# A Householder reduction interleaved with graph layers: other scalars, a later schedule, a plainer end of the turns

## The reference, cut to what matters

```python
# layer 0
h = relu(einsum('ts,bsh->bth', adj, x @ Wg0 + bg0))
h = relu(einsum('ts,bsh->bth', adj, h @ Wg1 + bg1))
for p in range(1, MAX_SKIP + 1):          # four LSTMs, over windows of p = 1, 2, 3, 4 rows
    wins = h[:, :nw * p, :].reshape(Bv * nw, p, Hd)
    last = _lstm_last(Wih[p-1], Whh[p-1], bih[p-1], bhh[p-1], wins)
    h = h.at[:, idx, :].set(last.reshape(Bv, nw, Hd))
# layer 3
L_norm = d_inv_sqrt[:, None] * (jnp.diag(deg) - A) * d_inv_sqrt[None, :]   # 64 x 64
_, U = jnp.linalg.eigh(L_norm)
```

## Time and profile before

| | |
|---|---|
| median of three runs | 2053.51 us (2052.98 to 2054.70) |
| the profiled execution | 2054.7 us, span 2051.8 us |
| PE busy | 1932.2 us, 94% of the span |
| DVE busy | 1520.7 us, 74% |
| ACT busy | 1153.5 us, 56% |
| POOL busy | 707.7 us, 34% |
| mean granted clock of TensorE | 0.972 |

### The profile page before, as it was taken

One profiled execution on the slowest core, in us unless ns is written; L12 is line 12 of the kernel. 1 busy time (PEld: TensorE's weight loads), 2 busy tenths in 40 slices (PEclk: granted clock), 3 DMA queues, 4 the chain that ended last, 5 costly groups with the idle time before them and its releaser, 6 DMA issues. The chain is left out here.

```text
span 2051.8 us, 32793 instructions
## 1 busy us (share of the span) xinstructions
PE 1932.2 (94%) x11833; PEld 1640.5 (80%) x11833; DVE 1520.7 (74%) x4011; ACT 1153.5 (56%) x1803; POOL 707.7 (34%) x1676
## 2 busy tenths in 40 slices
PE   6999999999999999999999989989699899699996
PEld 6888888888889999987887778867599534479895
DVE  5888776566566776888888879868566589789575
ACT  3555556445444445444344357647576588557575
POOL 2555552223233341000000155556544000108675
PEclk9999999999999999999999999999799999899898
DMA  2010101001000000010000043212222000004022
GB/s 95 22 31 22 52 22 42 1 1 41 1 1 1 1 1 1 1 42 1 1 0 1 1 129 113 73 31 93 72 73 71 3 1 1 11 24 134 22 73 82
DMA packets 65632, 71.16 MB, mean 35 GB/s; under 512 B 3767, under 2 KB 63294, under 8 KB 65470
## 3 DMA queue, kind: packets, MB, share of 16 engines
q1 hardware_dynamic: 65470, 69.07, 10.4%
HBM read 43.90 MB, written 25.17 MB: 34 GB/s over the span
## 5 line engine op out<-in xcount | busy, mean ns | idle before, releaser
L1977 ACT ACTIVATE l_gates<-l_acc,l_b 128x512 f32<-128x512 f32 (+1 forms) x408 | 240.4, 620 | 88.4 <-PE l_acc L475 86.5
L1875 ACT ACTIVATE l_x_hi<-hT 128x512 fp32r<-128x512 f32 (+1 forms) x144 | 101.1, 753 | 172.6 <-PE l_acc L475 172.1
L473 PE MATMUL l_acc<-l_x_hi,l_w1x_hi 128*128 128x336 f32 (+1 forms) x544 | 187.2, 344 | 3.2 <-ACT l_gates L1977 2.2
L475 PE MATMUL l_acc<-l_x_lo,l_w1x_hi 128*128 128x336 f32 (+1 forms) x544 | 188.1, 346 | 0.0
L474 PE MATMUL l_acc<-l_x_hi,l_w1x_lo 128*128 128x336 f32 (+1 forms) x544 | 188.0, 346 | 0.0
L473 PE MATMUL l_acc<-l_x_hi,l_w0x_hi 128*128 128x512 f32 x464 | 182.1, 392 | 5.5 <-ACT l_gates L1977 4.6
L474 PE MATMUL l_acc<-l_x_hi,l_w0x_lo 128*128 128x512 f32 x464 | 181.2, 391 | 0.0
L475 PE MATMUL l_acc<-l_x_lo,l_w0x_hi 128*128 128x512 f32 x464 | 181.2, 390 | 0.0
L1984 ACT ACTIVATE l_gates<-l_cell 128x512 f32<-128x512 f32 (+1 forms) x112 | 63.7, 569 | 191.1 <-DVE l_cell L2036 156.3
L244 POOL TENSOR_TENSOR bi_shifted<-bi_shifted 32x126 f32<-32x126 f32 (+61 forms) x62 | 17.7, 286 | 398.6 <-DVE bi_shifted L231 398.6
L1247 ACT ACTIVATE leaky<-sc_g 128x1024 f32<-128x1024 f32 x128 | 121.2, 1032 | 21.8 <-PE sc_g L1361 21.4
(11 more groups left out here) (519 smaller groups left out, 6328.5 us busy)
## 6 DMA issues: line engine op xcount, KB each, us to landing
xin<-in_x SPq DMA_DIRECT2D x16, 512.0 KB, 3.8
hidB<-in_x SPq DMA_DIRECT2D x16, 512.0 KB, 5.0
x<-hT SPq DMA_DIRECT2D x16, 512.0 KB, 3.1
hidB<-x SPq DMA_DIRECT2D x16, 512.0 KB, 3.9
x<-hidB SPq DMA_DIRECT2D x16, 512.0 KB, 2.9
attention_residual<-x SPq DMA_DIRECT2D x16, 512.0 KB, 3.9
out_x<-hT SPq DMA_DIRECT2D x16, 512.0 KB, 2.9
l_rawx<-in_wih SPq DMA_DIRECT2D x4, 1024.0 KB, 5.7
```

The lines of the kernel that those rows point to most:

```text
L473: t.matmul(out, left[0], right[0], start=start, stop=False)
L475: return t.matmul(out, left[0], right[1], start=False, stop=stop)
L1875: i = nc.scalar.activation(as_windows(xs[s % 2][0][:, ch, 0:bg * nw], nw), cols(p, bg, nw, group, k, ch), ACT.Copy)
L1977: i = a.activation(gates[:, j, q, 0:n], acc[:, j, q, 0:n], FUNC[q], bias=b[:, o:o + 1])
```

## The change

Three things are changed. In the reflections, DVE's front has three operations fewer (the sign, the flag and the norm) and signals `begun` as soon as the sum of squares is there; POOL's `scalars` has 13 operations instead of 9, all 13 of them up to `scaled`, where it was 8; the flag has one place instead of two. In the schedule, the first reflection is issued in half 1 of turn 2 instead of half 0, and 30 instead of 29 are issued in the turns, the last in half 0 of turn 17. In the last turns, the order of `rows_high`/`rows_low` and `tanh`/`hidden` is the same as in all other turns.

```diff
--- before.py
+++ after.py
@@ -156,8 +156,7 @@
         self.w, self.pr = (t[0:self.Q, :, :].rearrange("p a f -> p (a f)") for t in (bi.chain, bi.other))
         self.vb_col, self.w_col = take(2, self.Q), take(2, self.Q)
         self.update, self.z, self.p = take(2, N), take(16), [take(4), take(4)]
-        self.tail, self.norm, self.den, self.sign = (self.z[:, n:n + 1] for n in (0, 1, 2, 7))
-        self.flag = [self.z[:, n:n + 1] for n in (3, 15)]
+        self.tail, self.x1x1, self.den, self.flag = (self.z[:, n:n + 1] for n in range(4))
         self.rows = bi.rows
 
     def bind(self, sem):
@@ -165,36 +164,35 @@
             "begun", "scalars", "applied", "basis"))
 
     def front(self, v, dve, k):
-
 
         s, lo, x = self.on_dve, k + 1, self.v[k % 2]
         h = lo // self.Q
         if k > 1:
             dve.wait_ge(self.rotated, k - 1)
         s.after(v.transpose(x[:, h * self.Q:], self.A[:, h:, k:k + 1].to_broadcast([self.Q, 2 - h, self.Q])))
-        x1 = x[:, lo:lo + 1]
-        s.add(v.tensor_tensor_reduce(self.prod[:, lo + 1:], x[:, lo + 1:], x[:, lo + 1:], 1.0, 1e-35,
-                                     ALU.mult, ALU.add, self.tail))
-        s.after(v.tensor_scalar(self.sign, x1, 0.0, 2.0, ALU.is_ge, ALU.mult))
-        s.after(v.tensor_scalar(self.flag[k % 2], self.tail, 1e-35, -1.0, ALU.is_gt, ALU.mult))
-        v.tensor_scalar(self.norm, x1, x1, self.tail, ALU.mult, ALU.add).then_inc(self.begun, 1)
+        v.tensor_tensor_reduce(self.prod[:, lo + 1:], x[:, lo + 1:], x[:, lo + 1:], 1.0, 1e-35,
+                               ALU.mult, ALU.add, self.tail).then_inc(self.begun, 1)
 
     def scalars(self, g, pool, k):
 
 
         s, z, lo = self.on_pool, self.z, k + 1
-        x1, norm, den, flag = self.v[k % 2][:, lo:lo + 1], self.norm, self.den, self.flag[k % 2]
-        y, t, root, r, e, half = (z[:, n:n + 1] for n in (4, 5, 6, 8, 9, 10))
+        x1, tail, norm, den, flag = self.v[k % 2][:, lo:lo + 1], self.tail, self.x1x1, self.den, self.flag
+        y, t, root, sign, r, u, half = (z[:, n:n + 1] for n in range(4, 11))
         pool.wait_ge(self.begun, k + 1)
-        s.add(g.tensor_scalar(e, flag, 1.0, x1, ALU.add, ALU.mult))
+        s.add(g.tensor_scalar(sign, x1, 0.0, 2.0, ALU.is_ge, ALU.mult))
+        s.after(g.tensor_scalar(norm, x1, x1, tail, ALU.mult, ALU.add))
+        s.add(g.tensor_scalar(flag, tail, 1e-35, -1.0, ALU.is_gt, ALU.mult))
         s.after(g.tensor_tensor(y, norm, half, ALU.pow))
+        s.add(g.tensor_scalar(root, y, norm, None, ALU.mult))
         s.after(g.tensor_scalar(t, y, y, norm, ALU.mult, ALU.mult))
         s.after(g.tensor_scalar(t, t, -0.5, 1.5, ALU.mult, ALU.add))
-        s.after(g.tensor_scalar(root, norm, y, t, ALU.mult, ALU.mult))
-        s.after(g.tensor_scalar(r, self.sign, -1.0, root, ALU.add, ALU.mult))
-        s.after(g.tensor_scalar(den, r, x1, norm, ALU.mult, ALU.add))
-        g.tensor_tensor(x1, x1, r, ALU.add).then_inc(self.scaled, 1)
-        s.after(g.tensor_scalar(self.rows[0:self.Q, 1, lo:lo + 1], r, flag, e, ALU.mult, ALU.add))
+        s.after(g.tensor_scalar(root, t, root, None, ALU.mult))
+        s.after(g.tensor_scalar(r, sign, -1.0, root, ALU.add, ALU.mult))
+        s.add(g.tensor_scalar(den, r, x1, norm, ALU.mult, ALU.add))
+        s.after(g.tensor_tensor(u, x1, r, ALU.add))
+        s.after(g.tensor_scalar(self.rows[0:self.Q, 1, lo:lo + 1], u, flag, x1, ALU.mult, ALU.add))
+        g.tensor_copy(x1, u).then_inc(self.scaled, 1)
 
     def back_products(self, v, dve, k):
 
@@ -207,7 +205,7 @@
         p, w = self.p[k % 2], N - lo
         s.after(v.tensor_tensor(self.products[:, h0:, lo:], self.AM[:, h0:, lo:],
                                 x[:, lo:].unsqueeze(1).to_broadcast([self.Q, 4 - h0, w]), ALU.mult))
-        s.add(v.tensor_scalar(self.z[:, 12:13], self.z[:, 11:12], self.flag[k % 2], None, ALU.mult))
+        s.add(v.tensor_scalar(self.z[:, 12:13], self.z[:, 11:12], self.flag, None, ALU.mult))
         s.after(v.tensor_reduce(p[:, h0:], self.products[:, h0:, lo:], AX.X, ALU.add))
         s.after(v.transpose(self.pr[:, h0 * self.Q:], p[:, h0:2].unsqueeze(2).to_broadcast([self.Q, 2 - h0, self.Q])))
         s.add(v.tensor_scalar(vb[:, lo:], x[:, lo:], self.z[:, 12:13], None, ALU.mult))
@@ -478,7 +476,7 @@
 BIAS_ROWS = 96
 BEHIND = 3
 
-REFLECTION_AT = {at: k for k, at in enumerate([(it, half) for it in range(2, 16) for half in range(2)] + [(16, 0)])}
+REFLECTION_AT = {at: k for k, at in enumerate([(2, 1)] + [(it, half) for it in range(3, 17) for half in range(2)] + [(17, 0)])}
 XBUFS = 2
 
 
@@ -1517,18 +1515,13 @@
                     input_high(it + 1)
                 if it - 1 < GROUPS:
                     second_high(it - 1)
-                if it == TURNS - 1:
-                    lstm.rows_high(act, g + 1)
                 if g >= 0:
                     lstm.gates(act, g, 0)
-                if 0 <= g < GROUPS - 2:
                     lstm.tanh(act, g, 0)
                 if 0 <= it - 2 < GROUPS:
                     rows_out(it - 2)
-                if 0 <= g + 1 < GROUPS:
+                if g + 1 >= 0:
                     lstm.rows_high(act, g + 1)
-                if g >= GROUPS - 2:
-                    lstm.tanh(act, g, 0)
                 if it < GROUPS:
                     first_high(it)
                 if g >= 0:
@@ -1602,19 +1595,15 @@
                 reflection((it, 0))
                 if it - 1 < GROUPS:
                     second_low(it - 1)
-                if it == TURNS - 1:
-                    lstm.rows_low(dve, g + 1)
                 if g >= 0:
                     lstm.cell(dve, g, 0)
                 if it + 1 < GROUPS:
                     input_low(it + 1)
-                if 0 <= g < GROUPS - 2:
+                if g >= 0:
                     lstm.hidden(dve, g, 0)
                 reflection((it, 1))
-                if 0 <= g + 1 < GROUPS:
+                if g + 1 >= 0:
                     lstm.rows_low(dve, g + 1)
-                if g >= GROUPS - 2:
-                    lstm.hidden(dve, g, 0)
                 if it < GROUPS:
                     first_low(it)
                 if g >= 0:
```

## The result

The changed kernel takes 2082.11 us (median of four runs, 2081.22 to 2083.29), the kernel before 2053.61 on the same measure. The ratio is 1.0139, with a 95% interval of 1.0121 to 1.0156: 28.5 us slower. The forecast was 15.9 us slower with a range that ended at 2081. The direction was right, the size was not, and the time lies just above the range.

A forecast was written before the change was run, and what follows sets the result against it. PE bounded the turns before; after, DVE and POOL's loop would, at 21.2 us against 20.27. Terms 11.4 - 4.1 + 4.4 + 4.5 + 1.7 - 2 = +15.9 us on 2054.7 give 2070.6, median 2069.4 us; range 2056 to 2081.

The forecast's parts named there:

- The bound: In the middle turns: DVE and POOL together become the bound, a loop of 21.2 us against PE's 20.27.
- The turns: Turns 4 to 16: the longer loop costs 0.9 us a turn, +11.4 us over 12 turns, bounds +1 and +20.
- X: DVE's stretch from a front's end to the next reciprocal, with `rows_low`, `first_low`, cell, hidden, `mixed_low`: 6.0 us before, 6.65 forecast.
- Y: DVE's stretch between reflections with `second_low`, cell, `input_low` and hidden: 5.5 us before, 6.85 forecast.
- if the flag is caught already: Upper case for Y: POOL's flag, ahead of `pow`, is held by DVE's SBUF operations, making Y 7.1 us.
- the second rival: In the turns, POOL is caught more often: loop 21.8 us, +20 there, 2079 us in all; chance 0.14.
- The start: Up to turn 4: with the reflection ahead of `second_low` in turn 2 gone, -4.1 us stay (-3.5 to -4.6).
- too short for the clock: PE's stop of 2.36 us at 56.65 shrinks to about 1.1, without half clock behind it, saving another 1.7.
- The end of the turns: Late reflections delay `rows_low` of groups 14 and 15: PE stops 4.4 and 4.5 us, plus 1.7 at half clock.
- The LSTMs: Behind the turns: PE's stops at rounds' ends move to other units and nearly cancel, -2 us (-4 to 0).
- gets out of the way: Last unit of the fourth LSTM, where 10 bisection steps fall away: part of the -2 us for the LSTMs.

The follow-up runs named there:

- short scalars: Changed kernel's schedule and order with the reflections' scalars of the kernel before: 1.0037, +7.6 us against the kernel before.
- the late start: Kernel before without the reflection ahead of `second_low` in turn 2, half 0, 28 in the turns: 0.9993, and 0.9998 when run again.
- the kernel with the ending short: Changed kernel with POOL's second half as before, 11 operations up to `scaled` instead of 13, no copy: 1.0061, +12.5 us against the kernel before.

## Why the prediction was wrong in size

**The bound: right.** DVE and POOL together are the bound in the turns. Both stretches wait for POOL, and PE waits for `h_lo`. Adding operations on POOL alone brings the long turns, and taking some off brings most of the short ones back.

**The turns: the step that failed.** I wrote "I get 6.2 if pow isn't caught, 7.0 if everything is. I take 6.65" for X and "with the hand-over 6.85" for Y, and a loop of 21.2 us. Measured in a middle turn are 6.89 and 7.20, and 2 x 3.79 + 6.89 + 7.20 = 21.67 us. Both ends had been worked out (X 7.0; "if the flag is caught already, 7.1"), and I chose between them by the assumption that `pow` would be the one caught, just as the cell starts.

What failed is the time at which POOL reaches `pow`. Sign, norm and flag had 0.75 us from the first start to that of `pow`; where nothing holds them they take 0.94 (228.28 to 229.22). The cell was put at 1.06 us behind the accumulator and starts at 1.07. The flag starts at 1.00 and would run to 1.23. By the prediction's own figures it would have run to 1.13, so it was in flight there too when the cell began, and the prediction went past that. When `pow` is caught its own work is over when the hold ends; when the flag is, `pow` is still to come. Late in the turns the reflections are shorter, the flag gets through, and `pow` is the one held:
```profile
303.06 0.23 POOL L185 TENSOR_SCALAR bi_shifted<-bi_shifted 32x1 f32<-32x1 f32 x1
303.37 2.67 POOL L186 TENSOR_TENSOR bi_shifted<-bi_shifted 32x1 f32<-32x1 f32 x1
```
Y takes 6.89 us in that turn. So the forecast's 6.85 was right for the case that it assumed, and the case was another until then; the price is 0.3 us a turn. X is longer by 0.24 for the same reason: `pow` is reached at 2.38 us instead of 2.1, 0.11 behind the start of the cell. Putting the flag behind `pow` does not win the 0.3 back in Y, since the flag's own time then falls behind the hold. That one operation is held until hidden's end, and that most of a chain then follows, sets the bulk of Y in every case.

The loop of the second rival (21.8) is what the turns show, and its "+20" is the measured +18.7. By the spans the sum was missed by 11.2 us (27.1 less 15.9), and 7.3 of them lie here. The forecast had 0.9 us for each of twelve turns, with an allowance for the first. Eleven of them became 1.5 us longer on average. The twelfth, from turn 15 to 16, was only 17.68 us for PE before and takes 19.87, 2.2 more: the loop did not shrink with PE's work.

The first turns are the other part. The reflection is longer there, and X takes 7.17 since the flag is held in it too, for 0.9 us. So three turns take 22.3 to 22.4, and the turn does not come near 21.5 until the second half. I had 0.25 us a reflection for this.

**The start: nearly right, with two terms wrong.** -3.4 for -4.1. The forecast let PE get 6.7 us ahead, 3.4 of them from two half-clock stretches that would go. Neither gain came: the stop of 1.30 us, which was to be "too short for the clock", went along with 6.8 us at 1.2 GHz, as much as in both stretches before. The stops alone gave 2.19 and 1.06 us. The result hardly suffered, since the next `h_lo` comes a whole loop and a weight split later anyway, as the prediction said (23.4 us behind the one before; it had put 22.8).

**The end of the turns: right in place, mis-sized in parts.** +11.8 for +10.6. The stops were put at 4.4 and 4.5 us, and a half-clock stretch at 1.7. Measured are 4.9 more (5.90 less 0.98) and 2.15, with half-clock stretches of 6.8 and 3.4 us. The first begins within the stop, PE is busy for 6.1 and 3.4 us of them and loses half of that, 4.7: 11.8 in all. The second stop was forecast too long and the clock's part too small. With short scalars the two stops are 4.5 and 1.5 us. The reflection in turn 17 delays by the way predicted: with the old order its stop is gone and the end is 4.0 us shorter.

**The LSTMs: mis-sized.** -2 forecast, 0.0 in the two profiles. That stops would move to other units came out; that the last unit "gets out of the way" brought nothing that the profiles show.

**The sum of the parts.** Alone, the three parts cost 16.8, 2.1 and 1.2, together 20.1 us; the whole costs 28.5, 8.4 more, where the four intervals, taken as independent, leave about 6 open. Adding the schedule to the scalars brings 6.8 instead of 2.1, adding the order to both another 4.9 instead of 1.2. The intervals of these times overlap; that the order costs something here is read from the end of the turns, 48.0 us as against 44.0. A reflection at the end of the turns stands ahead of a low part that PE waits for, so a longer chain is paid there in full, while in the middle part of it is covered.

**What stays open.** Two runs of the late start could not show its 3.4 us at the start in the whole time, and the time of schedule with order has two clusters, 2058 and 2063, of which only the lower has a profile. What lets an operation of POOL get through beside DVE, and after which stop PE's clock falls, stay open as well; the rows are below.

## What to carry to other kernels

Add up the loop of the two engines that hand work to each other, against the busiest engine's turn, before calling either of them "idle": here DVE was 80% busy and POOL 57% in a turn, and the loop had some 0.5 to 1 us to spare. (This is an estimate from the kernel before with two operations added, some 1.1 us more in a turn: its turns go from 20.95 to 20.32 us, so 0.5 us of it were covered in the early turns and nearly all in the last.) Lengthening a chain on one of them is nearly free until the slack is used and then costs its full length each turn, so cost an edit at both ends, and give the dear one its weight where the row nearest to it (an operation held for 2.71 us) shows that it happens already. Parts that are harmless alone (a place at the end of the schedule, an order of the last turns) should be timed together with the part that makes their chain longer.

## What the runs showed of the hardware that I had not expected

A GpSimd operation on a 32x1 operand that starts just ahead of a VectorE operation with two SBUF inputs can be held until a whole run of such operations has ended: the flag at 216.85 for 2.57 us, over three operations of DVE (it takes 0.23 us otherwise), and with `pow` in its place, at 216.18, for 2.92 (otherwise 0.56). A head start of 0.07 or 0.08 us did not protect it. A longer one did in the same two kernels, over the turns before the last two. Flags and `pow`s that start 0.01 to 0.12 us ahead of the cell are all held, those of 0.13 to 0.16 us go either way, and from 0.17 us on, as with the `pow` at 228.39, all get through. But the head start alone does not decide it either. In the kernel before, this operation starts 0.32 us ahead of the cell (199.03) and takes 1.04 us instead of 0.33, and so in twelve turns one after the other.
```profile
198.71 1.04 POOL L191 TENSOR_SCALAR bi_shifted<-bi_shifted 32x1 f32<-32x1 f32 x1
```
The Trainium skill (SBUF — State Buffer, "SBUF: two separate sides") says that whichever of the two starts first gets the port pair for its whole instruction. By that rule the flag at 216.85 and `pow` at 216.18 would have ended in 0.2 and 0.6 us. The blocking between the engines agrees with the traces. The right of the first one agrees with them where the head start is 0.17 us or more in those two kernels, and not at 0.12 us or less, nor for L191. A start in the profile need not be the moment at which the operation takes the ports, and no run here shows that moment, so these rows do not refute the rule; they show that the order of two starts in a timeline is not enough to apply it.

PE's clock fell with shorter stops than I had thought possible. A stop of 1.24 us at 207.56 and one of 1.30 at 51.64 were followed by 3.4 and 6.8 us at 1.2 GHz, while the stop of 1.3 us at 185.8 was followed by none. Shorter ones had it too: 1.03 us at 272.45, and 0.64 us at 117.48 in the kernel with the ending short, both with 3.4 us behind them, while stops of 2.0 us in the kernel before (at 1099.11 and 1154.99) had none. By these rows the length of the stop alone does not decide it. Four stretches of 3.4 us at that clock lie in the turns of the changed kernel (98.8, 143.2, 208.0, 272.9) and none in those of the kernel before. They cost little there: the turns that begin at 207.6 and 272.4 with such a stretch take 21.9 us, the two between them 21.5, so about 0.4 us each instead of the 1.7 that the clock takes, since PE would have waited 1.0 us and more.
